# Second expert stage: GpSimd's send of a unit's second result tile also waits for a later unit's SiLU

## What is computed

```python
# per token, x of 128 features; H = 176 hidden; E = 8 experts, top 2
h  = silu((x @ w1[e] + b1[e]) * (x @ w3[e] + b3[e]))
oe = h @ w2[e] + b2[e]
y  = sum(weight[token, e] * oe for the token's two experts)
z  = the same network with shared weights, for every token
out = x + y + z
```

## Time and profile before

| What | us |
|---|---|
| Median of 3 runs (lowest, highest) | 693.52 (693.27, 696.43) |
| Span of the profiled execution, first to last instruction | 763.9 |
| Stage from the first send on, of that span | 618 to 764 |
| TensorE's busy time in the span | 671.5 (88%) |
| VectorE, ScalarE, GpSimd | 523.5, 415.8, 504.9 |

### The profile page before, as it was taken

The page is one execution under the profiler, slowest core; times in us unless marked ns, Lnnn a source line. Parts: engine busy times, 40 slices in busy tenths (PEclk is TensorE's granted clock), DMA queues, the critical chain, the costliest instruction groups (busy, mean ns, idle before and its releaser), DMA issues.

```text
span 763.9 us, 21054 instructions
## 1 busy us (share of the span) xinstructions
PE 671.5 (88%) x7092; PEld 546.5 (72%) x7092; DVE 523.5 (69%) x1515; ACT 415.8 (54%) x1158; POOL 504.9 (66%) x837
## 2 busy tenths in 40 slices
PE   8799998888876999999979999888888668788797
PEld 7567666665646999999957776666667568778787
DVE  5489988888663446555358898888886555555556
ACT  5477767654542434444447777656547445555563
POOL 5975788577564678877677778777667635455451
PEclk9899999999997999999979999999989989899999
DMA  5470000001331522343110101111211312222264
GB/s 166 124 305 2 17 27 27 27 30 36 137 99 48 160 70 81 97 127 89 46 36 29 30 26 40 54 37 37 66 34 37 89 51 77 61 75 72 75 232 152
DMA packets 45406, 57.78 MB, mean 76 GB/s; under 512 B 11379, under 2 KB 37142, under 8 KB 44630
## 3 DMA queue, kind: packets, MB, share of 16 engines
q1 hardware_dynamic: 36086, 38.17, 16.6%
q0 software_dynamic: 8640, 17.97, 7.1%
q10 hardware_dynamic: 576, 0.29, 0.1%
HBM read 33.82 MB, written 22.08 MB: 73 GB/s over the span
## 4 chain that ended last, share of the span: by engine, by line
PE 50%; POOL 17%; issue 12%; DVE 8%; ACT 5%; another core or an unknown queue 4%; DMA 2%; SPq 1%; DVEq 0%; POOLq 0%; ACTq 0%
POOL results L1625 9%; PE ptp L1349 8%; PE M L1366 7%; PE ptp L2078 6%; PE S L1326 5%; PE S L2059 5%; PE S L1330 3%; PE ptp L1352 3%; POOL xi L1618 2%; POOL rows L626 2%; PE M L1374 2%; PE M L1418 2%; PE S L2065 1%; SPq L707 1%
## 5 line engine op out<-in xcount | busy, mean ns | idle before, releaser
L626 POOL DMA_INDIRECT rows<-out_rows,posi x128 | 126.9, 991 | 50.1 <-issue 32.1
L806 ACT ACTIVATE pT<-ptp 128x512 f32<-128x512 f32 (+1 forms) x192 | 95.1, 525 | 97.7 <-PE ptp L1349 87.0
L1929 POOL DMA_INDIRECT results<-early,xs x71 | 69.0, 971 | 68.4 <-DVE early L2001 50.9
L1064 DVE TENSOR_REDUCE mx<-S 128x16 f32<-128x1232 f32 x64 | 91.3, 1427 | 18.3 <-PE S L1330 16.4
L1625 POOL DMA_INDIRECT results<-early,xi x71 | 75.9, 1069 | 40.5 <-DVE early L1687 35.1
L1065 DVE TENSOR_TENSOR pr<-S,mx 128x1232 f32<-128x1232 f32 x64 | 92.3, 1442 | 2.2
L1724 PE MATMUL S<-first_w,early 128*128 x568 | 77.2, 279 | 3.0 <-DVE early L1687 1.5
L1714 PE MATMUL S<-early,w1s 128*128 128x128 f32 x568 | 76.9, 279 | 0.6 <-ACT early L1659 0.6
L1366 PE MATMUL M<-pT,vm 128*32 128x128 f32 (+1 forms) x2048 | 74.7, 283 | 1.1 <-ACT pT L806 0.6
L1349 PE MATMUL ptp<-cst,pr 128*128 128x128 f32 x512 | 74.0, 290 | 0.0
L1724 PEld LDWEIGHTS S<-first_w,early 128*128 128x128 f32 x568 | 69.5, 193 | 5.9 <-issue 5.7
(11 more groups left out here) (221 smaller groups left out, 1527.9 us busy)
## 6 DMA issues: line engine op xcount, KB each, us to landing
xs<-rows SPq DMA_DIRECT2D x142, 66.0 KB
first_w<-in_e_W SPq DMA_DIRECT2D x2, 2048.0 KB, 8.2
swap<-results SPq DMA_DIRECT2D x32, 128.0 KB
first_w<-results SPq DMA_DIRECT2D x6, 512.0 KB
rows<-out_rows,posi POOLq DMA_INDIRECT x128
x_res<-in_x SPq DMA_DIRECT2D x1, 1536.0 KB, 8.4
W1r<-in_e_W SPq DMA_DIRECT2D x1, 1536.0 KB, 10.8
out_x<-x_res SPq DMA_DIRECT2D x3, 512.0 KB, 2.7
```

Source lines behind the costliest of these rows:

```text
L626: nc.gpsimd.indirect_dma_start(rows[:, :], bass.IndirectOffsetOnAxis(posi[:, k, n:n + 1], 0), out_rows[:, ring_slot(groups, n), k, :], Non ...
L806: nc.scalar.activation(pT[0:rows_of, G * r:G * r + count, :], ptp[q % 2][0:rows_of, 0:count, :], ACT.Exp, scale=SCALE)\
L1064: do(V.tensor_reduce(mx[:, :].rearrange("p (g j) -> p g j", g=G), sc, AX.X, ALU.max))
```

## The change

The send of a unit's first tile is as before. Ahead of the second tile's send GpSimd now also waits for `hT_ready` to reach u + 4, that is, for the SiLU of unit u + 3 (shared units count too). This holds for all 35 routed units that have two tiles, since unit u + 3 exists for each of them. No instruction is removed, and the order of the sends stays.

```diff
--- before.py
+++ after.py
@@ -1928,8 +1928,13 @@
             pool.wait_ge(ys_ready, i + 1)
             nc.gpsimd.indirect_dma_start(results[:, :], bass.IndirectOffsetOnAxis(place, 0), ys[:, s, :], None).then_inc(ys_out[s], 16)
 
-        for i in range(SLOTS):
-            send(i)
+        for u in range(NU):
+            if not is_routed(u):
+                continue
+            for at, i in enumerate(tiles_of(u)):
+                if at and live(u + 3):
+                    pool.wait_ge(hT_ready, u + 4)
+                send(i)
 
     def scalar(act):
         act.wait_ge(st["weights_in"], st["n_weights"])
```

## The result

The changed kernel takes 697.18 us (median of 20 runs, 694.88 to 699.89) against 695.25 us (693.0 to 697.42, 20 runs) for the kernel before on the same chip: a ratio of 1.003, 95% interval 1.0017 to 1.0042. By the ratio that is 2.1 us slower. It is inside the prediction's range and less than the 0.5% that it took for the least change to be told, but no change, which it forecast, lies outside the interval.

What follows compares the result with a forecast made beforehand. TensorE was taken as nearest to the bound, GpSimd's send queue nearly equal at undisturbed flow. The terms, each 0 us, summed to 0 us, so 693.5 us was forecast, with a range of 687.5 to 698.8 us.

Steps and rivals of the forecast that it cites:

- The forecast of no change: Whole kernel: the sends shift without effect on the time, 693.5 us; 0.54 for a result within 3.5 us of that.
- the one on SyncE's loads: Loads into buffers freed by sends: the tightest, tile 51, has 3.2 us left for a 1.3 us shift, so 0 us.
- bound of 2.7 us for the landing: Tile loads: landing has no row, so 2.7 us, the time of the larger stores, was taken as upper bound.
- 0.4 us would come out, once: Tile 51's load: what a shift of 3.6 us there, in place of 1.3 us, would cost.
- 35 waits, 0 us: GpSimd's queue: 35 more wait instructions fall into its 68.4 us of idle time and cost 0 us.
- the rival of the met wait: GpSimd's second sends: without holes they come after their SiLU anyway, so the change does nothing, 693.5 us; chance 0.08.
- The result buffers, the end and VectorE's copies, 0 us each: Buffer reuse, last sends and weight copies beside sends: 0 us each, with up to +1.4 us at the end, +1 for copies.
- Both rivals with a measurable effect: Sends beside late completions: faster, holes end a send sooner, 688.4 us, chance 0.27; slower, longer send rows, 698.6 us, 0.19.
- the nameless holes: ScalarE's copy of hidden products: eight waits, 23.8 us, with matmul completions some 2 us late beside four sends in a row.
- the account of the 3.15 us: Stretch from 618 to 741 us: 39 units take 3.15 us each, against 2.45 us for TensorE at full flow.
- the slower one: GpSimd's sends: those held back lengthen the next row, half of eight holes grow by 1.27 us, 698.6 us; chance 0.19.
- The choice to put the holes down to the profiled execution: 763.9 us profiled against 693.5 us timed: the late completions were believed to belong mostly to the profiled execution.

Runs made afterwards that it cites:

- c4: The changed kernel measured again with no further edit: 698.44 us, ratio 1.0055 (1.0037 to 1.0073) to the kernel before.
- a1: The kernel before, unchanged, measured and profiled again: 696.11 us, ratio 1.0003 (0.9972 to 1.0034).
- b1: The changed kernel with 20 buffers for the loaded tiles in place of 16: 696.24 us, ratio 0.9997 to the kernel before.
- d1: The changed kernel with 20 tile buffers in place of 16, a second time in more rounds: 696.37 us, ratio 1.0005 to the kernel before.
- b2: The changed kernel with the wait moved to the SiLU of unit u + 4 and 20 tile buffers in place of 16: 702.17 us, one run.
- b3: The changed kernel without the wait in unit 7, the first routed one: 697.9 us, one run.

## Why the prediction was right and wrong

**The forecast of no change** did not hold. The range did, and the 2.1 us are below the 3.5 us that the prediction took for the least that can be told, but twenty runs tell them from nothing (1.0017 to 1.0042), and c4's 1.0055 is above that bound. The true value is 2 to 4 us. That the forecast came near is in part luck: the term that failed happened to be small with this gate, and is 22 us with the next one.

**The step that failed** is the one on SyncE's loads: "The tightest I found is tile 51 ... That leaves 3.2 us for a shift of 1.3 us: 0 us." It was read from the disturbed execution, in which TensorE stood still for 18.5 of 123 us and ran at a granted clock of 0.90. Each stop gives the loads time: tile 51's has 5.9 us in the earlier trace rows, and in a1 less than half of it:

```profile
636.45 0.33 SPq L1884 DMA_DIRECT2D xs<-rows  x1
...
639.10 0.38 PE L2045 MATMUL M<-cst,xs 128*128 128x128 f32 x2
```

With these 2.7 us and its own bound of 2.7 us for the landing the prediction would have had no slack at all. Tile 17's load, 6.7 us in the disturbed execution, has 3.2 us, less 1.9 us to land: 1.3 us of slack, and the shift of the load is 1.4 us. The shift had the right size; the slack was less than half of what I took. The bound of 2.7 us for the landing erred on the safe side by 0.8 us, and didn't help.

Tile 51 is still the tightest in a1, with tile 69 (2.7 us as well), and yet it loses nothing: in the changed kernel it has 3.1 us. What makes a load late is its lead less the shift of the one send that frees its buffer, and the shift is largest where GpSimd has just caught up, so that the gate really holds the send. That is so at the first unit (tile 0 goes 0.8 us after its result) and behind each shared unit between the routed ones (tiles 20, 36 and 52 do so too). The sends held next are those of tiles 1, 21, 37 and 53, which free the buffers of tiles 17, 37, 53 and 69. Tiles 37 and 53 had 5.1 and 5.6 us; 17 and 69 had 3.2 and 2.7, and these are the two places that lose in the changed kernel; in c4 there is a third, 0.39 us behind tile 37's transposes, whose load went out 3.5 us ahead (why that was too little isn't told). The prediction took a shift of 1.3 us for every send alike, and one tightest load.

**A price that was missing** is what a late tile costs. I wrote "0.4 us would come out, once", as if TensorE lost only the lateness of the tile. At tile 17 it lost 0.15 us by the tile and 0.8 us by two register loads behind it, which had been free. Those instructions were not in my sum at all.

**35 waits, 0 us:** right. b1 and d1 have all of them and lose nothing. The table of GpSimd's waits in the changed kernel, 580 to 694:

```profile
POOL results L1929 <- issue: 15.9, 52, 0.3
POOL results L1929 <- ACT kT L1964: 9.4, 12, 1.5
POOL results L1929 <- DVE early L2006: 6.6, 7, 3.0
```

Only 12 of the 35 gates are the last to open, and five of these 12 are no longer than the 0.30 us between any two sends; I had said that 32 SiLUs end later than their send and that about half of the waits would be put down to ScalarE. That was the disturbed trace again, and in part the gates' own work. At full flow GpSimd needs 2.53 us a unit and TensorE 2.45, and falls behind slowly: in a1 the second send comes after its SiLU in only 12 of the 35 units. That is as far as the rival of the met wait goes without the gate. With it, the first send that is held moves all behind it, and these then find their SiLU done, so that two thirds of the waits are met. Where GpSimd has caught up, as at tile 20 (sent 0.8 us after its result in both kernels), the next gate still shifts all that follow: tile 21 goes 2.9 us after its result in place of 1.8.

**The result buffers, the end and VectorE's copies, 0 us each:** right in the sum. VectorE's wait for a send that hasn't landed grew from 0.2 us in one place to 1.6 in three, near the end, and the SiLUs show no loss there; b2 and b3 show how near this is. The last send went 96.8 us after the first one in place of 93.6, 3.2 us later where I had 1.3 to 1.7, and TensorE's part at the end didn't wait for it.

**Both rivals with a measurable effect** rested on the nameless holes. There are none in the stretch in a1 or in the changed kernel, so neither could happen. One more reading was off: in the 123 us of the earlier trace rows 36 units pass, not 39, so they took 3.4 us each, and part of that is the granted clock of 0.90, which I left out of the account of the 3.15 us. The result's sign is that of the slower one, but not its mechanism. **The choice to put the holes down to the profiled execution** was right, and the rule weighed beside it was no explanation. The Trainium skill's page "NOTIFIC — the notification-queue block", section 7.1, says that the block's inner path holds its producers back rather than lose a record; nothing of the kind shows in the other profiled executions: a1's took 695.81 us by its own time beside a median of 696.11, and that of the changed kernel was the quickest of 20. With section 10, by which a record costs the engine no cycles, these traces agree. What disturbed the one execution of 763.9 us no run shows.

## What to carry to other kernels

Before a slack is read from a profile, compare its span with the timed runs: a trace that is 10% long shows slack that isn't there, above all for transfers that run ahead in a ring of buffers. Of every load, not only of the tightest, take its lead ahead of its reader, less the time to land, less the shift of the very send that frees its buffer; here the shift was largest behind each place where the in-order queue had caught up. A wait that becomes real in an in-order queue costs also whatever small instructions stand behind it and were hidden by the queue's lead; put register loads ahead of the wait.

## What the runs showed of the hardware

A register load on TensorE's queue takes 0.30 us in the median of the changed kernel and 0.49 at most, and two of them in a row left the array idle for up to 0.71 us where the queue had no lead. The 66 KB load lands in 1.9 us in the median (1.7 to 2.9 in the changed kernel) and the scattering send of a tile in 2.4 us (2.2 to 6.3). The price of the gate at units u + 2, u + 3 and u + 4 was 0, 2 and 22 us: it was free until it had used up the ring's slack, and at tile 17 that was 1.3 us with 16 buffers. In the run with u + 4 the granted clock fell twice after TensorE had stood for 1.7 to 1.8 us, and twelve matmuls then took 2.70 us in place of 1.50.
